# A decoder layer's expert stage takes its normed rows from the attention stage: stored by each batch, fetched and transposed during the last cross attention

## The reference, cut to what matters

```
x = x + self_attn(layernorm(x))                 # 16 heads of 32: 6 plain, 4 hyperbolic, 6 cosine; causal
x = x + cross_attn(layernorm(x), ctx, mask)     # 16 heads, 750 context rows a batch
x = x + experts(layernorm(x))                   # over all 1792 rows

def experts(x):                                 # product keys, 8 heads
    q = batchnorm(x @ w_q)                      # mean and variance over all 1792 rows
    sim = q . keys                              # 2 halves x 8 heads x 128 keys
    best 8 of each half, best 8 of their 64 sums -> indices into 16384 experts, softmax gates
    h = gate * gelu(x . down[index]);  out = sum over heads and picks of h * up[index]
```

## Time and profile before

| | |
|---|---|
| timed runs | 2706.38, 2709.6, 2710.87 us, median 2709.6 |
| profiled execution | 2701.66 us, its span 2699.9 us |
| border from attention to experts | 1411.2 us |
| busy: PE, DVE, ACT, POOL | 88%, 69%, 44%, 42% of the span |

### The profile page before, as it was taken

One profiled execution on the slowest core, in us unless ns is written; L12 is line 12 of the kernel. 1 busy time (PEld: TensorE's weight loads), 2 busy tenths in 40 slices (PEclk: granted clock), 3 DMA queues, 4 the chain that ended last, 5 costly groups with the idle time before them and its releaser, 6 DMA issues. The chain is left out here.

```text
span 2699.9 us, 37982 instructions
## 1 busy us (share of the span) xinstructions
PE 2374.3 (88%) x12584; PEld 1274.5 (47%) x12584; DVE 1849.5 (69%) x5421; ACT 1193.3 (44%) x3236; POOL 1133.8 (42%) x1097
## 2 busy tenths in 40 slices
PE   6899999999999999999767799898988888897776
PEld 3455565555656556565544344344434434343222
DVE  3476765766657576675645897877778687878555
ACT  1457374673736647365443243343334333433322
POOL 2121111212112121111002676777777777777775
PEclk9899999999999999999778899999999999999999
DMA  5000001000010000100002999999999999999998
GB/s 177 8 24 15 24 2 37 1 15 24 2 37 1 15 24 5 34 1 8 1 33 68 370 384 355 403 398 407 385 407 398 395 397 406 400 392 404 404 411 349
DMA packets 158050, 514.38 MB, mean 191 GB/s; under 512 B 16960, under 2 KB 27200, under 8 KB 157856
## 3 DMA queue, kind: packets, MB, share of 16 engines
q0 software_dynamic: 129024, 469.82, 44.3%
q1 hardware_dynamic: 27248, 40.62, 4.5%
q10 hardware_dynamic: 1584, 1.52, 0.2%
HBM read 504.56 MB, written 7.34 MB: 190 GB/s over the span
## 5 line engine op out<-in xcount | busy, mean ns | idle before, releaser
L1519 POOL DMA_INDIRECT e_rows<-in_experts,e_idx x896 | 894.1, 998 | 343.7 <-issue 287.7
L1573 PE MATMUL e_ps_out<-e_rows,e_diag 128*128 128x512 f32 x1792 | 836.7, 612 | 151.6 <-ACT e_diag L1848 151.4
L1737 DVE CUSTOM_DVE_ANT_0 e_rows<-e_rows,xn_all 128x512 f32<-128x512 f32 x896 | 567.0, 688 | 242.1 <-DMA e_rows<-in_experts,e_idx 241.5
L1573 PEld LDWEIGHTS e_ps_out<-e_rows,e_diag 128*128 128x128 f32 x1792 | 339.4, 195 | 599.8 <-issue 431.1
L1848 ACT ACTIVATE e_diag<-ident_f,e_weight 128x128 f32<-128x128 f32 x896 | 286.2, 390 | 306.7 <-DVE e_weight L1748 300.4
L915 DVE SCALAR_TENSOR_TENSOR ring<-ps_s,mask 112x750 f32<-112x750 f32 x256 | 232.7, 935 | 149.4 <-PE ps_s L525 113.8
L1099 ACT ACTIVATE ring<-ring,neg_max 112x750 f32<-112x750 f32 x256 | 233.4, 913 | 164.0 <-DVE neg_max L925 164.0
L536 PE MATMUL ps_t<-ident,ring 112*125 112x112 f32 x1536 | 232.9, 290 | 46.5 <-ACT prob_t L1112 37.1
L536 PEld LDWEIGHTS ps_t<-ident,ring 112*125 112x125 f32 x1536 | 198.1, 195 | 123.5 <-ACT ring L1099 59.1
L1843 ACT ACTIVATE e_active<-e_hidden 128x4 f32<-128x4 f32 x224 | 46.0, 205 | 467.7 <-DVE e_hidden L1737 467.4
L1112 ACT COPY prob_t<-ps_t 125x336 f32<-125x336 f32 x512 | 200.0, 440 | 98.6 <-PE ps_t L536 98.2
(11 more groups left out here) (184 smaller groups left out, 2882.8 us busy)
## 6 DMA issues: line engine op xcount, KB each, us to landing
e_rows<-in_experts,e_idx POOLq DMA_INDIRECT x896, 6.7
ctx_t<-in_ctx_t SPq DMA_DIRECT2D x8, 1500.0 KB, 6.5
e_w_q<-in_ffn_wq SPq DMA_DIRECT2D x16, 256.0 KB, 7.0
x_in<-in_x SPq DMA_DIRECT2D x8, 448.0 KB, 3.6
x_dram<-x SPq DMA_DIRECT2D x8, 448.0 KB, 3.1
acc<-x_dram SPq DMA_DIRECT2D x7, 512.0 KB, 6.8
out<-acc SPq DMA_DIRECT2D x14, 256.0 KB, 6.0
w_qkv<-in_w_qkv_t SPq DMA_DIRECT2D x3, 1024.0 KB, 10.3
```

Of the source, the lines that this page charges most:

```text
L1519: pool.indirect_dma_start(rows[:, v % RING, k, :], None, table[:, :], bass.IndirectOffsetOnAxis(ap=idx[:, e:e + 1], axis=0))\
L1573: mm = nc.tensor.matmul(ps_out[t % 2][:], diag[:, HU * (v % ND) + k, :], rows[:, v % RING, k, D:], start=(s == 0 and k == 0), stop=(s == S ...
L1737: last = nc.vector.tensor_tensor_reduce(down, down, xn_all[:, t, :], 1.0, 0.0, ALU.mult, ALU.add, hidden[:, b, k:k + 1])
```

## The change: the norm is made in attention, and 12 tiles are fetched and turned ahead

`AHEAD_TILES` is 12: the tiles of 128 rows that lie wholly in the first seven batches. Each of these batches norms its x2 in the next batch's self attention and stores it to a second DRAM tensor, `x2n_dram`. The large tensors of the experts are allocated first, and attention's tensors lie in them as views: w_qkv and x_in in `acc`; w_proj, w_q, w_k and v_s in `xn_all`; ctx_t, qk and rot in `xn_t`; keys_t in a new `w_in`, which later holds the experts' weights. Once the last batch no longer needs them, SP fetches 12 tiles of x2 and 12 of normed rows and the first weights over them, and PE and ACT turn two tiles in each of the quads 2 to 7 of the last cross attention, through the PSUM bank `ps_y`. The expert block fetches, norms and turns only tiles 12 and 13.

```
+AHEAD_TILES = (B - 1) * S // P // 2 * 2
...
+        acc_flat = acc[:].rearrange("p n d -> p (n d)")
...
+        w_qkv = acc_flat[:, 0:3 * KC * D].rearrange("p (c n) -> p c n", c=KC)
+        x_in = acc_flat[0:TT, 3 * KC * D:3 * KC * D + NT * D].rearrange("p (t d) -> p t d", t=NT)
...
+        x2_n = flat[:, 0:NT * D].rearrange("p (t d) -> p t d", t=NT)
...
+            def store_normed(b):
+
+                sp.wait_ge(x2n_ready.sem, x2n_ready.at(b, NT))
+                sp.dma_start(batch_of(x2n_v, b), x2_n).then_inc(x2n_stored.sem, 16)
+
+            def experts_in():
+
+                sp.wait_ge(qkv_done.sem, qkv_done.at(last, 3 * NT))
+                sp.wait_ge(x2_stored.sem, 16 * B)
+                for g in range(AHEAD_TILES // 2):
+                    n = slice(2 * g, 2 * g + 2)
+                    sp.dma_start(acc[:, n, :], x2_dram.rearrange("(n p) d -> p n d", p=P)[:, n, :]).then_inc(acc_in, 16)
+                sp.wait_ge(q2_done.sem, q2_done.at(last, KC))
+                sp.wait_ge(x2n_stored.sem, 16 * (B - 1))
+                for g in range(AHEAD_TILES // 2):
+                    n = slice(2 * g, 2 * g + 2)
+                    sp.dma_start(xn_all[:, n, :], x2n_dram.rearrange("(n p) d -> p n d", p=P)[:, n, :])\
+                        .then_inc(xn_in[g], 16)
...
             for b in range(B - 2):
                 store(b)
+                store_normed(b)
                 next_inputs(b + 1)
             store(B - 2)
+            store_normed(B - 2)
+            experts_in()
             store(B - 1)
...
+            def turn_ahead(n):
+
+                pe.wait_ge(xn_in[n // 2], 16)
+                if n == 0:
+                    pe.wait_ge(v_ready.sem, v_ready.at(last, NC))
+                else:
+                    pe.wait_ge(xt_ready, n)
+                for c in range(KC):
+                    mm = nc.tensor.transpose(ps_y[:, c * P:(c + 1) * P], xn_all[:, n, c * P:(c + 1) * P], ident[:])
+                mm.then_inc(xt_turned, 1)
...
                         front(following, q, 2 * half)
+                        if q >= 2 and following is None:
+                            turn_ahead(2 * (q - 2) + half)
                         if q >= 2 and half == 0:
                             cross_weigh(b, q - 2)
...
+            def output_stats(b):
+
+                for t in range(NT):
+                    nc.vector.bn_stats(stats[:, t, :], x2[:, t, :])
+                nc.vector.drain()
+                for t in range(NT):
+                    nc.vector.bn_aggr(mean_var[:, t, :], stats[:, t, :])
+                nc.vector.drain()
+                nc.vector.tensor_scalar(var_eps[:], mean_var[:, :, 1], LN_EPS, None, ALU.add)\
+                    .then_inc(x2_var_ready.sem, 1)
+
+            def output_normed(b):
+
+                dve.wait_ge(x2_rstd_ready.sem, x2_rstd_ready.at(b, 1))
+                for t in range(NT):
+                    nc.vector.tensor_scalar(x2_n[:, t, :], x2[:, t, :], mean_var[:, t, 0:1], rstd[:, t:t + 1],
+                                            ALU.subtract, ALU.mult).then_inc(x2n_ready.sem, 1)
...
                 elif 3 <= s < NC + 1:
                     values_out(b, s - 2)
+                if s == 3 and prev is not None:
+                    output_stats(prev)
+                if s == NC and prev is not None:
+                    output_normed(prev)
...
             def cross(b, following):
 
+                if b >= 1:
+                    dve.wait_ge(x2n_stored.sem, x2n_stored.at(b - 1, 16))
...
+            def turned_ahead(n):
+
+                act.wait_ge(xt_turned, n + 1)
+                nc.scalar.copy(xn_t[:, :, n * P:(n + 1) * P], ps_y[:].rearrange("p (c n) -> p c n", c=KC)).then_inc(xt_ready, 1)
...
                         if q >= 1 and place in (0, 2):
                             cross_turned(b, 4 * q - 4 + place)
+                        if q >= 2 and place in (0, 2) and following is None:
+                            turned_ahead(2 * (q - 2) + place // 2)
...
+                if prev is not None:
+                    pool.wait_ge(x2_var_ready.sem, x2_var_ready.at(prev, 1))
+                    nc.gpsimd.tensor_tensor(rstd[:], var_eps[:], minus_half[:], ALU.pow).then_inc(x2_rstd_ready.sem, 1)
...
-            for g in range(3):
-                x2_group(g)
+            x2_group(AHEAD_TILES // 2)
             block_in(0, 0)
-            for g in range(3, NTF // 2):
-                x2_group(g)
...
             def first_head():
 
                 pe.wait_ge(ident_made, 2)
-                done = 0
                 for c in range(QC):
-                    for n in range(done, chunk_tiles(c)):
-                        turn(n)
-                    done = chunk_tiles(c)
+                    if chunk_tiles(c) > AHEAD_TILES:
+                        for n in range(AHEAD_TILES, NTF):
+                            turn(n)
                     for part in range(2):
                         project(0, 0, 2 * c + part)
...
             def first_head():
 
-                count_at = {4: 0, 6: 1}
-                for g in range(NTF // 2 + 1):
-                    if g < NTF // 2:
-                        row_sums(g)
-                    if g >= 1:
-                        row_norm(g - 1)
-                    if g in count_at:
-                        count(0, 0, count_at[g])
-                for c in (2, 3):
+                row_sums(AHEAD_TILES // 2)
+                count(0, 0, 0)
+                row_norm(AHEAD_TILES // 2)
+                for c in (1, 2, 3):
                     count(0, 0, c)
```

More of the change, by code:

```diff
@@ L93, with build_attention @@
 FRONT_FIRST = ((5, 0), (6, 0))
-def build_attention(nc, a, x2_dram):
+def build_attention(nc, a, x2_dram, x2n_dram, acc, xn_all, xn_t, w_in):
     with ExitStack() as ctx:
@@ L269, in build_attention @@
         x2_stored = steps("x2_stored", 16)
+        x2_var_ready = steps("x2_var_ready", 1)
+        x2_rstd_ready = steps("x2_rstd_ready", 1)
+        x2n_ready = steps("x2n_ready", NT)
+        x2n_stored = steps("x2n_stored", 16)
+        acc_in = sem("acc_in")
+        first_w_in = sem("first_w_in")
+        xn_in = [sem(f"xn_in{g}") for g in range(AHEAD_TILES // 2)]
+        xt_turned = sem("xt_turned")
+        xt_ready = sem("xt_ready")
         def head_rows_of(h):
@@ L1254, with build_experts @@
 PIECES = ((0, FIRST_TILES), (FIRST_TILES, NTF))
-def build_experts(nc, a, out, x2_dram, acc, xn_all, xn_t, ident):
+def build_experts(nc, a, out, x2_dram, acc, xn_all, xn_t, w_in, ident):
     with ExitStack() as ctx:
@@ L1317, in build_experts @@
         ps_out = [psum(f"ps_out{i}", [P, 512]) for i in range(2)]
-        x2_in = [sem(f"x2_in{g}") for g in range(NTF // 2)]
+        x2_in = sem("x2_in")
         ident_made = sem("ident_made")
@@ L1444, in x2_group @@
                 n = slice(2 * g, 2 * g + 2)
-                sp.dma_start(acc[:, n, :], x2_v[:, n, :]).then_inc(x2_in[g], 16)
+                sp.dma_start(acc[:, n, :], x2_v[:, n, :]).then_inc(x2_in, 16)
             w_v = a["ffn_wq"].rearrange("(c p) (f n) -> f p c n", p=P, n=KD)
@@ L1451, in block_in @@
                 f = head + half * HF
[L1452 to L1453 removed]
+                if head > 0 or half > 0:
+                    src = w_v[bass.ds(f, 1)].rearrange("o p c n -> (o p) c n")
+                    sp.dma_start(w_q[:, half], src).then_inc(w_loaded[half], 16)
                 src = k_v[bass.ds(f, 1)].rearrange("o p n -> (o p) n")
                 sp.dma_start(keys[:, half], src).then_inc(w_loaded[half], 16)
[L1457 to L1458 removed]
+            x2_group(AHEAD_TILES // 2)
             block_in(0, 0)
[L1460 to L1461 removed]
             sp.dma_start(gamma[:], a["gamma"]).then_inc(small_in, 16)
@@ L1485, in _ @@
                 .then_inc(iota_ready, 1)
-            for g in range(NTF // 2):
-                n = slice(2 * g, 2 * g + 2)
+            for g in range(1):
+                n = slice(AHEAD_TILES, NTF)
                 pool.wait_ge(row_var_ready, g + 1)
@@ L1527, in project @@
                 n, c, part = nth(head, half), i // 2, i % 2
-                if i == 0:
-                    pe.wait_ge(w_loaded[half], 32 * head + 32)
+                if i == 0 and n >= 1:
+                    pe.wait_ge(w_loaded[half], 32 * head + 16 * (1 + half))
                 if part == 0:
                     if n == 0:
-                        pe.wait_ge(xn_t_ready, chunk_tiles(c))
+                        if chunk_tiles(c) > AHEAD_TILES:
+                            pe.wait_ge(xn_t_ready, chunk_tiles(c) - AHEAD_TILES)
                     elif n == 1 and c < 2:
-                        pe.wait_ge(xn_t_ready, NTF)
+                        pe.wait_ge(xn_t_ready, NTF - AHEAD_TILES)
                     elif n == 1:
@@ L1550, in match_keys @@
                 n = nth(head, half)
+                if n == 0 and g == 0:
+                    pe.wait_ge(w_loaded[0], 16)
                 pe.wait_ge(q_ready, QC * n + -(-P * TPB * (g + 1) // QN))
@@ L1865, in first_head @@
```

(6 more changed lines are left out.)

45 lines of the change are left out of this document (25 added, 20 removed).

## The result

The changed kernel takes **2684.5 us** (median of five timed executions) against 2709.6, a ratio of 0.99 with a 95% interval of 0.9884 to 0.9917: 25 us faster. Forecast were 2703.0 us and a range of 2691 to 2716, so the sign was right and the size was not: the gain is almost four times the forecast one and lies outside the range. One of the five executions took 2992.95 us at a mean granted clock of 0.777 and is left out of the ratio; the other four go from 2674.53 to 2684.68 us, with a median of 2684.0.

The account below looks back on a forecast made before the run. Heads were taken as limited by PE, VectorE searches and gathers, passing on the experts' earlier start. Start -21.8, norm +7.6, clock +3.4, turns +4.2 give -6.6 us: 2703.0 us against the median 2709.6, range 2691 to 2716.

Parts of the forecast that it names:

- a shift of 1449.2: Start of experts: the fourth projection's end, 1449.2 us, moves earlier and the whole shift reaches the kernel's end.
- Part 1, the start: Start of experts: three of four projections run at once, the fourth ends at 1427.4 instead of 1449.2; gain 21.8 us.
- My 3 us: First expert projections: PE runs at half rate for L = 3 us before full clock returns, costing 1.5 us.
- Part 2, the norm: Seven self attentions: the added norm puts 1.08 us each on the path, 7.6 us; bounds 0 and 11.
- The statistics: Self attention, VectorE step 3: 1.76 us of statistics, cost 0, at most 0.5 if the 0.2 us cover fails.
- The two norms: Self attention, VectorE step 6: two tensor-scalars of 0.542 us, 1.08 us on the path before PE's last self turn.
- The clock in the tails: Ends of self attentions: longer PE pauses add one more clock fall, 3.4 us; bounds -8.8 and +13.
- Rival C: Self attention ends: the clock falls in every batch, +3.0 us against before (2712.6), up to +28; chance 0.18.
- Rival B: Clock holds: last cross attention's slow quads turn fast, tails lose nothing more; -17.8 us, 2691.8 us; chance 0.17.
- Part 3, the turns: Last cross attention, quads 2 to 7: twelve added turns cost 4.2 us; bounds 0 and 9.3.
- three slow quads of 1.15 each: Last cross attention: quads alternate, three at half clock lose 1.15 us each, the other three 0.25 each.

Follow-up runs that it names:

- the second trace of before: The unchanged kernel before, run once more for a second profile: 2710.09 us, heads 1225.4 us.
- the two slower series: Two series of padded kernels and the changed kernel with 128 bytes, in which the kernel before itself took 2854 us; ratios 0.9961 to 1.0013.
- counter-test: The changed kernel with 128 unused bytes ahead of the gathered rows, bringing their start back to a multiple of 512 bytes: 2695.38 us, 0.996 to the kernel before.

## Why the prediction was wrong, point by point

**The step that failed** is in the first paragraph: "From there heads are limited by PE, VectorE searches and gathers, all counted from that start, so I let a shift of 1449.2 pass to the end one for one." The shift did pass (24.3 us timed, 20.3 in the traces). But that sentence also took the heads' own length as fixed. It changed by -13.1 us (-16.3 against the second trace of before), because the new `w_in`, allocated ahead of the gathered rows, moved them and the smaller tensors behind them from a multiple of 512 bytes to 384 bytes beyond one. Padding alone in one direction gave -13.6 us, in the other +14. The change's description told of the placement, and my working gave it no term. The view that would have warned me was the stretch of the heads, with its DMA share of 1.00 at 392 GB/s: with the DMA engines full, 1% on a packet is some 1% of 1222 us.

Without the placement the change gives -12.4 us (the interval goes from -14.6 to -7.0) where I summed -6.6. The terms:

**Part 1, the start.** Forecast -21.8; -20.3 in the traces, -24.3 timed. The fourth projection ended 17.7 us after the border instead of the 16.2 that I had, because the low clock lasted longer: 24 matmuls took 12.07 us, 3.04 above full speed, so about 6.1 us at half rate instead of 3. The stretches show it:

```profile
1422.00:1425.00 3.00, 2.58 (x4) 1.34 (x5) 0.00 (x0) 0.00 (x0) 0.40 (x2) 0.50 0.67 207
1425.00:1428.00 3.00, 3.00 (x6) 1.34 (x5) 1.70 (x5) 0.00 (x0) 0.65 (x1) 0.50 0.38 107
1428.00:1431.00 3.00, 3.00 (x10) 1.51 (x9) 1.08 (x2) 0.81 (x1) 0.50 (x3) 0.99 0.00 0
```

PE is granted 0.50 (1.2 GHz) until 1428 and 0.99 from there, after having idled from 1417.4 to 1422.4. My 3 us was counted in the trace of before from the first projection, behind transposes. The Trainium skill (TensorE: Matmul & The Clock Gate, Part 4: PE-mode transpose) says that transposes don't count as PE activity in the same way. Counted from the first projection, the clock came back after 3 us there and 6.1 here; counted from the first work of PE, transposes included, after 8.3 there and 6.1 here. Neither count repeats, so the two traces don't settle what transposes count for.

**Part 2, the norm.** In the timeline of the last batch's self attention, as in the earlier trace rows:

```profile
1255.67 1.28 DVE L870 BATCH_NORM_STATS2 stats<-x 112x6 f32<-112x512 f32 x2
...
1257.56 0.39 DVE L906 CUSTOM_DVE_ANT_0 ring<-ps_s,causal 112x224 f32<-112x224 f32 x1
...
1260.62 0.69 DVE L840 TENSOR_TENSOR v_c<-ps_y,bv 125x512 f32<-125x512 f32 x1
```

```profile
1261.55 3.70 PE L506 MATMUL ps_y<-w_v,xn_t 128*125 128x512 f32 x8
...
1276.15 0.95 PE L541 MATMUL ps_t<-ident,ring 112*112 112x112 f32 x8 [1.07 <-ACT prob_t L1140]
```

The statistics are hidden as forecast: the eviction ends at 1261.31, PE's values group that needs it begins at 1261.55 with no wait, cover 0.24 us. The two norms of 540 ns are on the path: PE's last self turn idles 1.07 us where the earlier trace rows has 0.25. An interval without a fall of the clock is 164.15 us instead of 163.3: +0.85 a batch, forecast 1.08. Over seven batches that is 6, forecast 7.6. Timed, the norm alone against the placement alone is 0.0028 of 2709, 7.6 us, and 3.5 against the kernel padded ahead of the rows; those runs were on different chips, and the intervals leave some 5 us to either side.

**The clock in the tails.** Forecast +3.4 for one more fall. Over six times 164.15 the intervals of the changed kernel lie 9.1 us (8.8 before over 163.3): the falls are fewer but cost more each (169.5 and 167.8 stand for 5.4 and 3.7; the 163.7 that the prediction calls an interval without a fall is 0.4 above the cleanest). In these six nothing was added: +0.3. But the last batch's tail, which lies behind the last of these stores, did get slower. PE in the kernel before, the spreading of the sums, the output projection and the query projection (the last self turn at 1269.43 is in the earlier trace rows):

```profile
1271.88 2.03 PE L440 MATMUL ps_s<-inv_sum,head_rows 32*128 32x112 f32 x16
1273.84 8.82 PE L450 MATMUL ps_s<-w_proj,act_t 128*112 128x512 f32 x16
...
1291.49 7.73 PE L620 MATMUL ps_s<-act_t,w_q 128*128 128x224 f32 x32 [1.84 <-DVE act_t L697]
```

and in the changed one, where that turn begins at 1276.15:

```profile
1278.98 3.75 PE L481 MATMUL ps_s<-inv_sum,head_rows 32*128 32x112 f32 x16
1282.66 9.82 PE L491 MATMUL ps_s<-xn_all,act_t 128*112 128x512 f32 x16
...
1302.26 7.75 PE L661 MATMUL ps_s<-act_t,xn_all 128*128 128x224 f32 x32 [1.85 <-DVE act_t L752]
```

From the turn to the query projection it is 22.1 us before and 26.1 after: **+4.0**, on top of the norm, which stands ahead of the turn. The granted clock is 0.50 from 1280 to 1286 in the changed kernel; over the same work of the kernel before, from 1273.28 to 1279.28, its mean is 0.72. It is no accident of one trace: from the last of these stores to the first shift of the last cross attention, the five traces with the norm (outside the two slower series) take 65.3 to 65.4 us and the six without it 60.3 to 61.9. By these the fall costs 2.5 to 4.3 us beyond the norm's 0.85. The norm alone, without fetches, has the 65.4, so the fetches are not the cause. The clock thus cost 4.3 us in all, near the 3.4 forecast. Rival C (every tail falls) is refuted by four intervals of 164.15. Rival B wanted the tails to lose nothing more and the slow quads to turn fast; the last tail lost 4.0, and the quads below gained nothing.

**Part 3, the turns.** Forecast 4.2, bounds 0 to 9.3. Timed, one pair of runs gave 6.3 (give or take 4) and the other nothing (give or take 6). The timeline of the last cross attention, DVE's first shift of quads as in the earlier trace rows, first the last one of the kernel before, then seven of the changed one:

```profile
1380.05 0.93 DVE L925 CUSTOM_DVE_ANT_0 ring<-ring,mask_bias 112x750 f32<-112x750 f32 x1
```

```profile
1327.71 0.93 DVE L1002 CUSTOM_DVE_ANT_0 ring<-ring,mask_bias 112x750 f32<-112x750 f32 x1
...
1337.71 0.93 DVE L1002 CUSTOM_DVE_ANT_0 ring<-ring,mask_bias 112x750 f32<-112x750 f32 x1
...
1349.99 0.93 DVE L1002 CUSTOM_DVE_ANT_0 ring<-ring,mask_bias 112x750 f32<-112x750 f32 x1
...
1359.99 0.93 DVE L1002 CUSTOM_DVE_ANT_0 ring<-ring,mask_bias 112x750 f32<-112x750 f32 x1
...
1369.99 0.93 DVE L1002 CUSTOM_DVE_ANT_0 ring<-ring,mask_bias 112x750 f32<-112x750 f32 x1
...
1381.09 0.93 DVE L1002 CUSTOM_DVE_ANT_0 ring<-ring,mask_bias 112x750 f32<-112x750 f32 x1
...
1391.09 0.93 DVE L1002 CUSTOM_DVE_ANT_0 ring<-ring,mask_bias 112x750 f32<-112x750 f32 x1
```

Four of these six quads take 10.0 us, one 12.3 and one 11.1: 63.4 us together, against 63.1 for the same six before (1316.92 to 1380.05). In this trace the turns cost **0.3 us**; the mean granted clock over the six is 0.85, before it is 0.82. It isn't always so. In the traces with the turns but the start of before, and of the counter-test, four of the six take 11.5 to 12.3 us, at a granted clock of 0.80 in the mean: 67.5 us together, where the eight traces without turns (again outside the two slower series) have 63.1 to 65.3. There the turns cost 2 to 4 us, as forecast. The forecast of three slow quads of 1.15 each holds in neither. The stage from the last store to the border shows the same: 171.0 and 170.5 us in the two traces with the norm and no turns there, 170.8, 175.0 and 175.0 in the three with them.

So, by these two traces, the sum should have read: start -20.3, norm +6, clock +4.3, turns +0.3, placement -13.1, in all -22.8 us; the two spans differ by 23.0. Without the placement these terms come to -9.7, inside the interval of the counter-test's -12.4: the -6.6 of the forecast had the three costs 4.6 us too high (7.6 + 3.4 + 4.2 against 6 + 4.3 + 0.3), most of it the turns, and the start 1.5 us too good. Each of these stayed inside its bounds. The term that was missing did the rest.

## What to carry to other kernels

When a change moves the allocation of anything that a saturated DMA queue writes to, compare the changed kernel also with its placement undone by a few unused bytes: here about half the gain was the placement's, and the kernel before gets it from one line. Put a control with a known effect into every series; without it the two slower series would have been read as proof that the bytes don't matter. And cut both traces at the same marks and compare the lengths of all stages, above all of the one that "only shifts"; one pair of traces is not enough where the granted clock differs from run to run, as the quads show.

## What the runs showed of the hardware that I had not expected

In this kernel the speed of the gathers goes with where in a partition they write: rows of 2 x 512 floats begun at a multiple of 512 bytes took 148.1 to 148.6 ns a packet (five traces), begun 384 bytes beyond one 146.3 to 146.9 ns (six traces), 1.3% less. Only these two remainders were measured with the DMA engines full. The reason is open: no run looked at anything finer than the queue's share. The same kernel's heads took 1210.4 us in one series and 1365.4 in another (the 384 bytes ahead), 1222.7 and 1366.9 (the counter-test's kernel), with attention unchanged (clean intervals between stores of 163.3 us for the one kernel and 164.2 for the other, each in both series).

The Trainium skill (DMA: Bandwidth & Descriptors, Specifications) gives about 358 GB/s as a core's limit from HBM, half of what the stack yields to its two cores, and 435 GB/s as the ceiling of the fabric. Here, with one core at work, the heads ran at 390 to 396 GB/s outside the two slower series, above the first and below the second; neither tells of the 1% between two placements.
